# Local attention: the output projection once per four blocks of tokens, 512 columns wide

## The reference, cut to what matters

```
def attn_layer(x, Wqkv, qs, ksc, Wo):          # x: tokens x 128, Wqkv: 128 x 3072
    q, k, v = heads(x @ Wqkv)                  # 16 heads of 64
    q, k = rotary(l2norm(q) * qs), rotary(l2norm(k) * ksc)
    out = local_attention(q, k, v)             # window 32, looks one window back
    return out.reshape(b, n, 1024) @ Wo        # Wo: 1024 x 128

def ffn_layer(x, g, bln, W1, b1, W2, b2):
    xn = (x - mean) / sqrt(var + 1e-05) * g + bln
    a, gate = split(xn @ W1 + b1)              # 341 and 341
    return a * gelu(gate) @ W2 + b2

for l in range(6):
    x = shift_tokens(x); x = x + attn_layer(x, ...)
    x = shift_tokens(x); x = x + ffn_layer(x, ...)
```

## Time and profile before

| | |
|---|---|
| median of 3 runs | 4060.26 us (4059.45 to 4061.49) |
| the profiled execution | 4064.39 us |
| its span | 4062.2 us |
| this branch in the span | about 125 to 1856 us |
| PE busy, share of the span | 3684.0 us, 91% |
| DVE | 3048.9 us, 75% |
| ACT | 2526.8 us, 62% |
| POOL | 1248.0 us, 31% |
| granted TensorE clock, mean | 0.952 |

### The profile page before, as it was taken

How to read it: one execution, slowest core, us unless ns; L and a number is a source line. 1 busy time by engine, 2 the same in 40 slices (tenths; PEclk the granted TensorE clock), 3 DMA queues, 4 the chain that set the end, 5 groups by cost and what they waited for, 6 DMA issues and landing times.

```text
span 4062.2 us, 121711 instructions
## 1 busy us (share of the span) xinstructions
PE 3684.0 (91%) x50424; PEld 2024.2 (50%) x50424; DVE 3048.9 (75%) x5108; ACT 2526.8 (62%) x3810; POOL 1248.0 (31%) x1096
## 2 busy tenths in 40 slices
PE   6799999999999999998999999999988699999998
PEld 2365555555555555555644555555554233333333
DVE  7788988888888989875637666667676777777772
ACT  6456666666666666665435555655564476767775
POOL 0466665656556655641100000000002011111121
PEclk8899999999999999997589999999999799999999
DMA  2123222223223222221000000000001211111100
GB/s 74 32 65 81 67 68 76 70 64 81 73 64 86 66 72 74 70 63 28 22 1 3 4 5 4 4 4 2 4 7 41 94 21 21 21 21 21 26 2 11
DMA packets 84727, 163.75 MB, mean 40 GB/s; under 512 B 26648, under 2 KB 36552, under 8 KB 82912
## 3 DMA queue, kind: packets, MB, share of 16 engines
q1 hardware_dynamic: 83937, 155.06, 14.6%
q10 hardware_dynamic: 223, 0.61, 0.1%
HBM read 40.88 MB, written 8.52 MB: 12 GB/s over the span
## 4 chain that ended last, share of the span: by engine, by line
PE 39%; issue 23%; POOL 18%; DVE 11%; ACT 6%; POOLq 0%; DMA 0%; DVEq 0%; SPq 0%; ACTq 0%
POOL arena L1523 9%; POOL arena L1527 7%; PE banks L1863 6%; PE banks L3162 5%; PE banks L1826 3%; ACT arena L3307 2%; PE banks L1844 2%; DVE arena L2033 2%; PE banks L3120 2%; PE banks L3136 2%; PE banks L1882 2%; POOL arena L1507 2%; DVE arena L2052 1%; DVE arena L3390 1%; DVE arena L1372 1%
## 5 line engine op out<-in xcount | busy, mean ns | idle before, releaser
L3390 DVE TENSOR_REDUCE arena<-banks 128x2 f32<-128x1024 f32 x512 | 613.9, 1223 | 198.5 <-PE banks L3127 93.3
L3307 ACT ACTIVATE arena<-banks 128x1024 f32<-128x1024 f32 x512 | 521.0, 1024 | 216.9 <-PE banks L3143 104.7
L1523 POOL TENSOR_TENSOR arena<-arena 128x512 f32<-128x512 f32 x384 | 424.7, 1127 | 638.2 <-DVE arena L1381 630.7
L1527 POOL TENSOR_TENSOR arena<-arena 128x1024 f32<-128x1024 f32 x192 | 533.1, 2776 | 15.1
L2033 DVE CUSTOM_DVE_ANT_0 arena<-arena,banks 128x512 f32<-128x512 f32 (+3 forms) x640 | 361.8, 603 | 145.1 <-issue 140.0
L972 PE MATMUL banks<-arena 128*128 128x512 f32 x768 | 370.4, 627 | 27.1 <-issue 14.5
L1971 ACT ACTIVATE arena<-banks 128x512 f32<-128x512 f32 (+3 forms) x320 | 168.7, 527 | 339.8 <-PE banks L1845 338.6
L3162 PE MATMUL banks<-arena 128*32 128x256 f32 x4096 | 335.1, 394 | 13.4 <-issue 8.3
L1963 ACT ACTIVATE arena<-arena 128x128 f32<-128x128 f32 (+15 forms) x256 | 328.6, 1285 | 14.0 <-DVE arena L2045 9.7
L1826 PE MATMUL banks<-arena 64*128 64x512 f32 (+3 forms) x1280 | 319.9, 575 | 6.4 <-issue 4.3
L2115 POOL COPY arena<-arena 128x512 f32<-128x512 f32 x32 | 19.7, 615 | 995.4 <-DVE arena L2059 995.4
(11 more groups left out here) (451 smaller groups left out, 7556.5 us busy)
## 6 DMA issues: line engine op xcount, KB each, us to landing
arena<-arena SPq DMA_DIRECT2D x768, 64.0 KB
arena<-arena SPq DMA_DIRECT2D x96, 384.0 KB, 3.6
arena<-arena SPq DMA_DIRECT2D x104, 128.0 KB, 3.4
arena<-in_lf_wqkv SPq DMA_DIRECT2D x6, 1024.0 KB, 5.3
arena<-arena SPq DMA_DIRECT2D x8, 512.0 KB
arena<-features_k SPq DMA_DIRECT2D x30, 128.0 KB
arena<-features_q SPq DMA_DIRECT2D x15, 216.0 KB
arena<-in_lf_wqkv SPq DMA_DIRECT2D x6, 512.0 KB, 4.0
```

Source lines behind the costliest of these rows:

```text
L1523: nc.gpsimd.tensor_tensor(r[:, :, e * H2:(e + 1) * H2], q[:, j, :, (1 - e) * H2:(2 - e) * H2], s[:, j, 1, e * H2:(e + 1) * H2].unsqueeze(1 ...
L1527: nc.gpsimd.tensor_tensor(a, a, lf_rb, ALU.add).then_inc(S("lf_rot" + x), 1)
L3307: nc.scalar.activation(bi_PT[n % 4], PS[:, 2 * bi_slot("S", n):2 * bi_slot("S", n) + 2].rearrange("p a b -> p (a b)"), ACT.Exp).then_inc(S ...
L3390: nc.vector.tensor_reduce(bi_max[j % 2][:, t, :, c], PS[:, 2 * slot:2 * slot + 2], AX.X, ALU.max).then_inc(S("bi_mx"), 1)
```

## The change: what it does

`lf_OT` becomes one buffer of 8 x 512, and `keep_o` writes block `n` at columns `n % 4 * 128`. `project` now takes a chunk `c`: it runs in the steps with `j` = 3 alone, at the place where it stood, with eight matmuls of 512 columns into the whole of bank 5. `add` follows in the same step, 512 columns wide. In the tail the last chunk is projected in two parts, three blocks (384 columns) and the last block (128 columns). The waits on `lf_y2` and `lf_wo` count chunks instead of blocks. The feed-forward's three `lf_G` tiles and `lf_sx` move from the arena into the buffer `xn`, which frees the room for `lf_OT`.

```
+        lf_OT = arena.f32_3(8, CH)
+        lf_sx = ck(xn, 3)
+        lf_G = [ck(xn, m) for m in range(3)]
+        def lf_projected(s):
+            c, j = divmod(s - 4, 4)
+            return c, c >= 0 and j == 3
 # scores, first half
-                    if n >= 3:
-                        pe.wait_ge(S("lf_y2"), l * NB + (n - 2))
+                    if n >= 6 and n % 4 == 2:
+                        pe.wait_ge(S("lf_y2"), l * NCH + (n - 2) // 4)
+            def project(c, l, first=0, last=4):
+                n = 4 * c + last - 1
+                ...
+                pe.wait_ge(S("lf_ot"), l * NB + (n + 1))
+                if last - first == 4:
+                    pe.wait_ge(S("lf_kT"), l * NB + (n + 4))
+                ...
+                t = slice(first * P, last * P)
                 for p in range(8):
-                    m = nc.tensor.matmul(PS[:, 5, 0:P], lf_wo[:, p], lf_OT[n % 2][:, p], start=(p == 0), stop=(p == 7))
+                    m = nc.tensor.matmul(PS[:, 5, t], lf_wo[:, p], lf_OT[:, p, t], start=(p == 0), stop=(p == 7), skip_group_check=last - first < 4)
 # PE step
-                if lf_live(s - 4, end):
-                    project(s - 4, l, end)
+                if lf_projected(s)[1]:
+                    project(lf_projected(s)[0], l)
 # PE tail: project(NB-3), project(NB-2), project(NB-1) become
+                project(3, l, 0, 3)      # after both(2, 1, l)
+                project(3, l, 3, 4)      # after values(NB - 1)
 # ACT
-                if n >= 2:
-                    act.wait_ge(S("lf_wo"), l * NB + (n - 1))
+                if n >= 4:
+                    act.wait_ge(S("lf_wo"), l * NCH + n // 4)
-                act.wait_ge(S("lf_y2"), l * NB + (4 * c + 4))
+                act.wait_ge(S("lf_y2"), l * NCH + (c + 1))
 # DVE
+            def add(c, l, first=0, last=4):
+                ...
+                nc.vector.tensor_tensor(lf_y2[:, t], lf_y[:, t], PS[:, 5, first * P:last * P], ALU.add)...
```

More of the change, by code:

```diff
@@ L228, in program @@
         lf_Vs = [arena.f32(INNER) for _ in range(4)]
-        lf_OT = [arena.f32_3(8, P) for _ in range(2)]
+        lf_OT = arena.f32_3(8, CH)
         lf_y = arena.f32(T + 1)
@@ L232, in program @@
         lf_xc = arena.f32(CH)
-        lf_sx = arena.f32(CH)
-        lf_G = [arena.f32(CH) for _ in range(3)]
+        lf_sx = ck(xn, 3)
+        lf_G = [ck(xn, m) for m in range(3)]
         RL2 = 20
@@ L354, in step @@
                 if more and s == NB + 3:
-                    sp.wait_ge(S("lf_wo"), l * NB + NB)
+                    sp.wait_ge(S("lf_wo"), l * NCH + NCH)
                     lf_load_wo(sp, following)
@@ L1061, in values @@
                     m.then_inc(S("lf_pv"), 1)
-            def project(n, l, end):
-                if n % NB == 0:
-                    pe.wait_ge(S("lf_wo_in"), (l + n // NB) * 16 + 16)
+            def project(c, l, first=0, last=4):
+                n = 4 * c + last - 1
+                if c % NCH == 0:
+                    pe.wait_ge(S("lf_wo_in"), (l + c // NCH) * 16 + 16)
                 pe.wait_ge(S("lf_ot"), l * NB + (n + 1))
-                if lf_live(n + 3, end):
+                if last - first == 4:
                     pe.wait_ge(S("lf_kT"), l * NB + (n + 4))
-                elif lf_live(n + 2, end):
-                    pe.wait_ge(S("lf_sub"), l * NB + (n + 3))
-                else:
-                    pe.wait_ge(S("lf_y2"), l * NB + n)
+                elif last < 4:
+                    pe.wait_ge(S("lf_sub"), l * NB + NB)
+                else:
+                    pe.wait_ge(S("lf_begun"), 1)
+                t = slice(first * P, last * P)
                 for p in range(8):
-                    m = nc.tensor.matmul(PS[:, 5, 0:P], lf_wo[:, p], lf_OT[n % 2][:, p], start=(p == 0), stop=(p == 7))
-                m.then_inc(S("lf_wo"), 1)
+                    m = nc.tensor.matmul(PS[:, 5, t], lf_wo[:, p], lf_OT[:, p, t], start=(p == 0), stop=(p == 7), skip_group_check=last - first < 4)
+                m.then_inc(S("lf_wo" if last == 4 else "lf_wo_part"), 1)
             def mean(c, l, bank=6):
@@ L1160, in tail @@
                 both(2, 0, l)
-                project(NB - 3, l, True)
                 values_ready(NB - 2, l, True)
@@ L1165, in tail @@
                 both(2, 1, l)
-                project(NB - 2, l, True)
+                project(3, l, 0, 3)
                 pe.wait_ge(S("lf_h"), l * 12 + 7)
@@ L1171, in tail @@
                 values(NB - 1, l, 1)
-                project(NB - 1, l, True)
+                project(3, l, 3, 4)
                 pe.wait_ge(S("lf_h"), l * 12 + 8)
@@ L1244, in keep_o @@
                 act.wait_ge(S("lf_pv"), l * NB + (n + 1))
-                if n >= 2:
-                    act.wait_ge(S("lf_wo"), l * NB + (n - 1))
-                nc.scalar.activation(lf_OT[n % 2].rearrange("p a (w q) -> p w a q", q=2 * WIN), PS[:, 0:2].rearrange("p w (a q) -> p w a q", q=2 * WIN),
+                if n >= 4:
+                    act.wait_ge(S("lf_wo"), l * NCH + n // 4)
+                nc.scalar.activation(lf_OT[:, :, n % 4 * P:(n % 4 + 1) * P].rearrange("p a (w q) -> p w a q", q=2 * WIN), PS[:, 0:2].rearrange("p w (a q) -> p w a q", q=2 * WIN),
                                      ACT.Copy).then_inc(S("lf_ot"), 1)
             def shifted(c, l):
-                act.wait_ge(S("lf_y2"), l * NB + (4 * c + 4))
+                act.wait_ge(S("lf_y2"), l * NCH + (c + 1))
                 if c >= 1:
@@ L1407, in probs @@
                 nc.vector.transpose(lf_PT.rearrange("p a b -> p (a b)"), lf_E2.rearrange("p a b -> p (a b)")).then_inc(S("lf_pt"), 1)
[L1409 to L1412, removed]
+            def add(c, l, first=0, last=4):
+                f = c % NCH
+                if last == 4:
+                    dve.wait_ge(S("lf_wo"), l * NCH + (c + 1))
+                else:
+                    dve.wait_ge(S("lf_wo_part"), 1)
+                t = slice(1 + f * CH + first * P, 1 + f * CH + last * P)
+                nc.vector.tensor_tensor(lf_y2[:, t], lf_y[:, t], PS[:, 5, first * P:last * P], ALU.add).then_inc(S("lf_y2" if last == 4 else "lf_begun"), 1)
             def centre(c, l, bank=6):
@@ L1463, in step @@
                     probs(s - 2, l, end)
-                if lf_live(s - 4, end):
-                    add(s - 4, l)
+                if lf_projected(s)[1]:
+                    add(lf_projected(s)[0], l)
                 if s == 0:
@@ L1477, in tail @@
                 probs(NB - 1, l, True)
-                add(NB - 3, l)
                 product(2, 0, l, True)
@@ L1481, in tail @@
                 residual(1)
-                add(NB - 2, l)
+                add(3, l, 0, 3)
                 product(2, 1, l, True)
                 product(2, 2, l, True)
-                add(NB - 1, l)
+                add(3, l, 3, 4)
                 centre(3, l, 2)
```

## The result

| | before | after |
|---|---|---|
| median | 4060.88 us (4059.45 to 4062.43, 4 runs) | 4107.67 us (4103.95 to 4111.02, 4 runs) |
| the profiled execution | 4064.39 us | 4103.95 us |
| its span | 4062.2 us | 4101.6 us |
| granted clock, mean | 0.952 | 0.954 |

The change makes the kernel slower: ratio 1.0114, interval 1.0101 to 1.0128. The forecast was 4090 in a range of 4068 to 4116. The measured time lies in that range, but above the 4078 to 4102 that the forecast gave for itself.

The account below looks back on a forecast made before the run. B and C were taken as bound by the loop through PE holding the projection, A's last part by DVE. 17 x 1.5 + 5 x 1.3 = +32, ends -2: +30, median 4090; own range 4078 to 4102, widened to 4068 to 4116.

Parts of the forecast that it names:

- A: Step from one subtraction to the next, `j` 0 to 1: DVE binds, only `add` falls out, -0.17 us to 18.48.
- B: Step `j` 1 to 2, bound by the loop through PE with the projection: -1.83 us to 14.9, 0.1 added for ties.
- C: Step `j` 2 to 3, same pattern as B: -1.77 us to 14.8, 0.1 added for ties.
- D: Step `j` 3 to 0, last of the four in a period: wide projection uncovered, +5.04 us to 21.96.
- signs of being wrong: Forecast wrong if A comes out under 17.5, D under 21.5, or B or C stays above 15.5 us.
- the loop's end: In 5 of 22 periods PE stands about 3.8 us for instructions after `values`, ahead of `qk`: +1.3 us each.
- The ends: Stretch before the feed-forward starts, its fourth step, and the tail: net -2 us, with the tail taken as 0.
- the lead: Before the feed-forward, three projections go, 6 us back; fourth step gets the wide one, +4: net -2, from -5 to +3.
- ties: Rival: B and C at 15.4 and 15.3, margins with GpSimd, PE and copy DMAs lost, 18 us more, 4108; chance 20%.
- Throughput: Rival: PE is the bound, its 1.0 us less per period comes back, 22 us less, 4038; chance 9%.
- Balance: Rival: D's 5 us partly covered or DVE's floor lower, D at +3.8, 4060 to 4066; chance 7%.
- Clock: Rival: the clock falls in B and C, 1.6 us a fall, 44 falls, 70 us more, 4160; chance 6%.

Follow-up runs that it names:

- Run 12: The kernel before with the projections of A and D cut to one of eight matmuls, those of B and C in full: 4060.28 us, ratio 1.0008.
- runs 9 and 10: Four added DVE reductions of 256 elements a step, ahead of `inverse`: in the kernel after (9) 4284.03 us, in the kernel before (10) 4241.69 us.
- run 3: The kernel after with one of the eight matmuls of each wide projection: 3997.6 us, ratio 0.9854.
- run 2: The kernel before with one of the eight matmuls of each narrow projection, in all four steps: 4035.11 us, ratio 0.9936.
- run 6: The kernel before with two added DVE reductions of 256 elements ahead of `inverse` in every step: 4057.85 us, ratio 1.0002.
- run 1: The kernel before with only the `lf_G` and `lf_sx` tiles moved into the buffer `xn`: 4061.86 us, ratio 1.0004.
- run 4: The kernel after with each chunk's first block projected alone in A (128 columns), the other three together in D (384 columns): 4066.08 us, ratio 1.0022.
- run 7: The kernel after with the second `up` matmul of steps B to D moved between the two halves of `values`: 4109.15 us, ratio 1.012.

## Why the prediction was right, and where its sizes were off

- **What bounds each step: right, and shown.** A is bound by DVE; B and C by a loop through PE that is 1.7 to 1.9 longer than DVE's own work; D takes the wide projection in full. Run 12 shows the free ones, runs 9 and 10 that DVE is the floor of A, B and C, run 3 that D falls when the wide one shrinks. None of the signs of being wrong came: A is over 17.5, D over 21.5, B and C under 15.5. For B and C the change itself is the evidence; run 2, which should have given the same 1.7 to 1.9, gave 1.15 and 0.98.
- **A: -0.17 forecast, 0.0 measured** (median). The addition did go from A. But `normed` takes 1.57 instead of the 1.39 of the earlier trace rows: it came 0.18 earlier and ended at the same distance from the subtraction. GpSimd's rotation of queries runs from 701.23 for 3.22 us, to 704.45, and `normed` ends 0.56 behind it; before, 692.31 and 3.22 make 695.53, and `normed` ends at 696.09, 0.56 behind it too. So it is held by GpSimd as `probs` is in run 6. Runs 1 and 4 bear this out: both have the tiles in `xn`, so the buffers are not it, and both have a narrow addition in A. There `normed` takes 1.38 or 1.39 in most periods, against 1.56 or 1.57 in 17 of 22 after, and A is as long. The 0.18 that the addition leaves goes to GpSimd.
- **B and C: -1.83 and -1.77 less 0.1 each forecast, -1.86 and -1.67 measured** (medians). The margins with GpSimd and the queries held. Missing were two things that lift the means to B -1.66 and C -1.25: the pauses of PE in `values`, 13 in 20 periods after, 4 before, and a granted clock of 0.90 in two steps C.
- **D: +5.04 forecast, +5.12 measured** (median). The matmul is 0.885, not 0.86: 0.2 more. The addition is 0.65, not 0.69. Its steps at the loop's end pause as before, and four pauses of `values` that stood in D before are gone from it, so its mean grows by 4.89.
- **The sum.** 1.59 a period by the medians, 1.5 forecast: 22 x 1.59 = 35.0. Single steps bring 5.8 more, 40.8 in all against the forecast's 32: B and C lie 4 and 9 above what their medians give, 5.6 of this in the two steps at the lower clock, and D and A lie 5 and 3 under it. The forecast has the loop's end in 5 of the 22 periods; the traces show 4, which is worth 0.2 us. The ends bring -1.4 against -2, by accident: the lead was forecast at -2 and measured +2.0, with a first wide projection of 8.37 and not 6.9, the last step brings -2.9 where 0 was taken, and the stretch ahead of the branch happened to be 2.1 shorter.
- **From 39.4 to 46.8.** The profiled execution after is the fastest of its four, the one before is above all four of its kernel. The medians lie 46.8 apart. Single executions of one kernel spread over 24 us in run 1, so I count the difference of 7 as spread. The range holds the measured time only because it was widened for the *ties*, whose mechanism did not come: without them its top was 4102. That part is luck.
- **The rivals.** *Throughput* falls with A at 18.67 and with run 12. *Balance* falls with D. *Clock* falls as it was put, with 44 falls and 70 us: it is 1.00 in every step B and in 20 of 22 steps C. In the other two it comes, behind a pause of PE and not by the shorter work alone, and costs some 1.6 us in each `qk`. *Ties* gave 4108, which is what was measured, but not by its mechanism: it had B and C at 15.4 and 15.3 in every step, and they are 14.89 and 14.79 in most, with a few at 15.3 to 15.9 that hold a pause of PE at `values`, and the two at 17.5 and 17.6 that hold a pause and the lower clock.
- **What stays open.** What the pauses are and why they stand in just these steps: the profile shows no releaser, and that PE lacks instructions is argued, not shown. In the kernel after 10 of the 13 come back at the same instruction in every layer, some 290 us apart: with 11 matmul instructions of `values` left (355.27, 644.88, 936.06, 1225.35, 1516.48) and with one left (441.72, 731.25, 1022.27, 1311.58, 1602.60). That speaks for a place in the code, the rival of run 7. Their number grows when PE has less to do between the short matmuls (33 and 26 in run 2, 15 and 21 at the same lines in run 12); moving a matmul between the bursts (run 7) did not remove them. And no version tried beats the kernel before: the best one that bunches and computes the whole reference is run 4, at 1.0022.

## What to carry to other kernels

Price an operation by the step in which it stands: two of four equal projections cost nothing here, two cost nearly their length, and the total of PE's busy time fell by 27 us while the kernel became slower. Bunching work is worth it only where the bunch finds cover; here it took two free pieces and two at 1.8 us and made one of 5.1 of them. A test by removal in the free places (run 12) told this within 0.1 us a step by the medians. Removal in all four (run 2) gave only some six tenths of what B and C cost, with pauses in the place of the rest, and a test by adding work told nothing until the durations of the neighbours had been read as well.

## What the runs showed of the hardware

- **DVE and GpSimd wait for each other inside an instruction.** `probs` takes 1.23 when it starts clear of GpSimd, 1.88 when 0.8 of a GpSimd operation is left, 3.0 to 3.4 when the wide one (2.35) has started 0.04 to 0.42 before it; in each of these cases it ends 1.08 after GpSimd's. GpSimd's wide operation takes 2.35 clear and 3.2 when `probs` is ahead of it. DVE's reductions beside the same GpSimd operations keep their 1.21. The Trainium skill ("SBUF — State Buffer", Who interferes with whom) has this as a rule: a DVE instruction with two SBUF inputs and a GpSimd instruction that reads SBUF take the shared port pair exclusively, "Issue order, not op shape, decides who blocks". The rows agree with it.
- **A float32 matmul's price grows nearly with its columns:** 2.05 for eight of 128 columns, 5.43 for eight of 384, 7.15 for eight of 512. One wide projection is 0.8 us cheaper than four narrow ones (7.08 against 4 x 1.98) and 3.5 times as long as one of them.
- **PE can stand in the middle of a burst of short matmuls** with nothing to wait for that the profile shows: up to 1.5 us in run 2, up to 1.2 in the kernel after, in steps with some 300 matmul instructions. That it waits for its instructions there is a reading, not a finding.
- **The granted clock can fall behind such a pause:** in the kernel after two of the pauses (1.15 and 1.17 us) are followed by `qk` at 5.28 and 5.19 us instead of 3.70, with a clock of 0.70 in the first one's stretch; a pause of 1.16 at 441.72 is not (`qk` 3.67).
